# Third layer's projection in 64-row halves, with the group norm folded into its weights

## What is computed

```
def _L2_conv_ref(x, Wa1, ba1, Wa2, ba2, Wb1, bb1, Wb2, bb2, ln2_g, ln2_b, Wg, bg, Wz, bz):
    a = jax.nn.sigmoid((x @ Wa1 + ba1) * (x @ Wa2 + ba2))      # 64 -> 16 channels
    b = jax.nn.sigmoid((x @ Wb1 + bb1) * (x @ Wb2 + bb2))      # 64 -> 16 channels
    g = jax.nn.sigmoid(x @ Wg + bg)                            # 64 -> 64 channels
    z = jnp.einsum('bikc,bkjc->bijc', a, b)
    return g * (_ln(z, ln2_g, ln2_b) @ Wz + bz)
```

## Time and profile before

| | |
|---|---|
| median of 3 runs | 2089.22 us (2088.78 to 2090.52) |
| the profiled execution | 2091.39 us |
| its span (first to last instruction) | 2089.3 us |
| mean granted TensorE clock | 0.959 |
| busy: TensorE / VectorE / ScalarE / GpSimd | 1770.6 / 1319.1 / 1372.3 / 1031.0 us |
| fold of the third layer | about 1180 to 1189 us |
| projection of the third layer, first to last instruction | 1189.3 to 1311.0 us |

### The profile page before, as it was taken

One profiled execution on the slowest core, in us unless ns is written; L12 is line 12 of the kernel. 1 busy time (PEld: TensorE's weight loads), 2 busy tenths in 40 slices (PEclk: granted clock), 3 DMA queues, 4 the chain that ended last, 5 costly groups with the idle time before them and its releaser, 6 DMA issues. The chain is left out here.

```text
span 2089.3 us, 41026 instructions
## 1 busy us (share of the span) xinstructions
PE 1770.6 (85%) x10389; PEld 1045.5 (50%) x10389; DVE 1319.1 (63%) x2920; ACT 1372.3 (66%) x2541; POOL 1031.0 (49%) x1044
## 2 busy tenths in 40 slices
PE   0889997797998899985699799799799998699776
PEld 0444454685554444444355477643344444588533
DVE  7566666124763677775977388466377778344675
ACT  0577876365996777774599566477478787244554
POOL 0267678003991677786899200089122223000599
PEclk9999998898999999998899899999899999899999
DMA  7357876774996265647499666189557776845599
GB/s 327 124 184 236 245 232 216 271 297 169 365 367 235 97 189 168 193 135 264 146 357 366 231 226 207 35 321 385 175 157 227 237 236 216 296 174 228 193 398 373
DMA packets 326947, 496.15 MB, mean 237 GB/s; under 512 B 22828, under 2 KB 188463, under 8 KB 320439
## 3 DMA queue, kind: packets, MB, share of 16 engines
q1 hardware_dynamic: 326838, 494.93, 68.4%
HBM read 285.12 MB, written 197.13 MB: 231 GB/s over the span
## 5 line engine op out<-in xcount | busy, mean ns | idle before, releaser
L809 POOL TENSOR_TENSOR lo<-xn,hi 128x512 f16<-128x512 f32 x192 | 224.1, 1167 | 373.5 <-DVE hi L736 231.9
L601 PE MATMUL ps<-w_heads,hi 64*128 64x256 f16 x3072 | 292.8, 273 | 11.7 <-POOL lo L809 4.7
L1118 ACT ACTIVATE O<-ps 128x512 f32 (+1 forms) x144 | 151.7, 1054 | 189.3 <-PE ps L1042 189.3
L750 DVE SCALAR_TENSOR_TENSOR sig<-ps,largest,sig 128x512 f32<-128x512 f32 x256 | 180.7, 746 | 145.4 <-ACT sig L664 144.5
L664 ACT ACTIVATE sig<-ps,largest 128x512 f32<-128x512 f32 x384 | 246.1, 692 | 32.2 <-PE ps L601 23.3
L1355 POOL TENSOR_TENSOR shared<-O,out_rs 128x128 f32<-128x128 f32 (+1 forms) x112 | 76.3, 683 | 371.0 <-DVE out_rs L1255 370.0
L645 ACT ACTIVATE zs<-ps,shift 128x512 f32<-128x512 f32 x192 | 132.0, 687 | 192.9 <-PE ps L569 188.9
L601 PEld LDWEIGHTS ps<-w_heads,hi 64*128 64x128 f16 x3072 | 153.2, 95 | 169.3 <-DVE sig L750 67.0
L1403 PEld LDWEIGHTS ps<-ident,shared 128*128 128x128 f32 (+1 forms) x1024 | 120.2, 133 | 224.8 <-issue 96.8
L1403 PE MATMUL ps<-ident,shared 128*128 128x128 f32 (+1 forms) x1024 | 160.8, 282 | 76.6 <-POOL shared L1355 49.2
L601 PE MATMUL ps<-w_heads,lo 64*128 64x256 f16 x1536 | 212.8, 272 | 0.0
(11 more groups left out here) (168 smaller groups left out, 3787.6 us busy)
## 6 DMA issues: line engine op xcount, KB each, us to landing
shared<-left_right SPq DMA_DIRECT2D x34, 2048.0 KB, 12.0
shared<-gate SPq DMA_DIRECT2D x224, 256.0 KB, 4.6
gate<-gates SPq DMA_DIRECT2D x96, 512.0 KB, 2.9
x_dram<-shared SPq DMA_DIRECT2D x192, 256.0 KB, 4.3
shared<-x_dram SPq DMA_DIRECT2D x192, 256.0 KB, 4.7
xs<-x_dram SPq DMA_DIRECT2D x64, 512.0 KB, 4.2
left_right<-stage SPq DMA_DIRECT2D x64, 448.0 KB, 5.9
left_right<-shared SPq DMA_DIRECT2D x64, 448.0 KB, 5.9
```

What stands on the lines that cost most here:

```text
L601: last = pe.matmul(PAIR[row][:, g, kb * S:kb * S + S], tokens[half, q % 8, at:at + P], k["w_heads"][half, part, :], start=(step == 0), sto ...
L750: dve.scalar_tensor_tensor(dst, pair(row, 1), k["largest"][:, 1:2], factor, ALU.mult, ALU.mult).then_inc(pair_read.sem, 1)
L809: pool.tensor_tensor(lo[:, q % 8, :], xn[:, q % 2, :], hi[:, q % 8, :], ALU.subtract).then_inc(c["lo_done"].sem, 1)
L1118: act.activation(o_of(ch), ps[h % 4 // 2][:, h % 2, :].rearrange("p (b g i) -> p b g i", b=2, g=2), ACT.Copy).then_inc(c["o_copied"].sem, 1)
```

## The change

1. Token products as halves. The four products of 128 rows and 128 columns become eight of 64 rows and 64 columns: for each group of 128 tokens one with partitions 0 to 63 and one with 64 to 127, each half writing a PSUM bank of its own (`TILES` is now two half banks of `ps[0]` or of `ps[2]`). The weights' columns are reordered so that each 64 × 64 block stands on the diagonal, and the reads of L910 and L914 follow.
2. The affine step goes, with `xn` and its semaphore; TensorE reads `xs` itself and waits for its DMA. The slots of `xs` are now freed by the gate product.
3. The fold takes up scale and shift: `plain_weights` scales the weights' rows, and a new TensorE part `multiply_shift` multiplies the raw weights with the shift and adds the result to the projection's biases (a one-row product of 128 columns and a 128-row one into the same bank, instead of the 512-column one) and to the gate's bias (a one-column product). `plain_weights` now comes before the scaling of the output weights instead of after it.

```diff
+    def multiply_shift(self, pe):
+        k = self.k
+        pe.wait_ge(self.loaded.sem, self.loaded(16 * len(self.loads)))
+        pe.wait_ge(self.done.sem, self.done(7))
+        pe.matmul(self.P_PROJ[:, 0:P], k["one"][:], k["b_rows"][0:1, 0:P], start=True, stop=False)
+        pe.matmul(self.P_PROJ[:, 0:P], k["w_proj"][:, P:2 * P], k["w_raw"][:, 0:P], start=False, stop=True)
+        self.counted(pe.matmul(self.P_GATE[:, 0:1], k["w_raw"][:, CH:CH + P], self.shift, start=True, stop=True))

     def plain_weights(self, dve):
-        k, step, mm = self.k, self.step, self.mm
-        step(dve, dve.tensor_copy(k["w_proj"][:], k["w_raw"][:]))
+        k, step, mm, w = self.k, self.step, self.mm, self.k["w_proj"]
+        step(dve, dve.tensor_copy(w[:, P:2 * P], self.shift.to_broadcast([P, P])))
+        dve.wait_ge(self.loaded.sem, self.loaded(16 * len(self.loads)))
+        step(dve, dve.tensor_scalar(w[:, 0:P].rearrange("p (g x e) -> p g x e", g=2, x=2),
+                                    k["w_raw"][:, 0:P].rearrange("p (x g e) -> p g x e", g=2, x=2), self.scale, None, ALU.mult))
+        step(dve, dve.tensor_scalar(w[:, CH:CH + P], k["w_raw"][:, CH:CH + P], self.scale, None, ALU.mult))
         dve.wait_ge(mm.sem, mm(self.mm_of["plain_bias"]))
-        step(dve, dve.tensor_copy(k["mask"][:].rearrange("p g b i -> p (g b i)"), self.P_PROJ))
+        bias = self.P_PROJ[:, 0:P].rearrange("p (x g e) -> p g x e", g=2, x=2)
+        mask = k["mask"][:].rearrange("p g b i -> p (g b i)").rearrange("p (g t x e) -> p g t x e", g=2, t=4, x=2)
+        for g in range(2):
+            step(dve, dve.tensor_copy(mask[:, g], bias[:, g].unsqueeze(1).to_broadcast([P, 4, 2, P // 4])))
+        step(dve, dve.tensor_tensor(w[:, 2 * P:2 * P + 1], self.P_GATE[:, 0:1], k["vec"][:, V_GATE_B:V_GATE_B + 1], ALU.add))
...
-        xs, xn = sb("xs", [P, 8, CH]), sb("xn", [P, 4, CH])
-        TILES, GATE = [ps[0][:, q, :] for q in range(2)], [ps[1][:, q, :] for q in range(2)]
+        xs = sb("xs", [P, 8, CH])
+        TILES, GATE = [ps[bank][:, :, 0:S] for bank in (0, 2)], [ps[1][:, q, :] for q in range(2)]
...
-                sp.wait_ge(c["xn_done"].sem, c["xn_done"](m - 7))
+                sp.wait_ge(c["gate_mm_done"].sem, c["gate_mm_done"](m - 7))
...
-                    pe.wait_ge(c["xn_done"].sem, c["xn_done"](m + 1))
+                    load = c[f"x_in{q % 8}"]
+                    pe.wait_ge(load.sem, load(i * 32 + (q // 8 + 1) * 16))
                     pe.wait_ge(c["masked"].sem, c["masked"](m - 1))
                     for t in range(4):
-                        last = pe.matmul(TILES[q % 2][:, t * P:t * P + P], xn[:, q % 4, t * P:t * P + P],
-                                         k["w_proj"][:, 0:P], start=True, stop=True)
+                        for g in range(2):
+                            half = slice(g * C, g * C + C)
+                            last = pe.matmul(TILES[q % 2][:, g, t * C:t * C + C], xs[half, q % 8, t * P:t * P + P],
+                                             k["w_proj"][half, half], start=True, stop=True)
                     last.then_inc(c["proj_done"].sem, 1)
                     pe.wait_ge(c["gate_done"].sem, c["gate_done"](m - 1))
-                    pe.matmul(GATE[q % 2], k["w_proj"][:, CH:CH + P], xn[:, q % 4, :],
+                    pe.matmul(GATE[q % 2], k["w_proj"][:, CH:CH + P], xs[:, q % 8, :],
                               start=True, stop=True).then_inc(c["gate_mm_done"].sem, 1)
...
-                dve.tensor_tensor(biased[:, q % 2].rearrange("p a b -> p (a b)"), TILES[q % 2],
-                                  k["mask"][:].rearrange("p g b i -> p (g b i)"), ALU.add).then_inc(c["masked"].sem, 1)
+                dve.tensor_tensor(biased[:, q % 2].rearrange("p (g e) -> p g e", g=2), TILES[q % 2],
+                                  k["mask"][:].rearrange("p g b i -> p g (b i)"), ALU.add).then_inc(c["masked"].sem, 1)
...
-                dve.tensor_tensor(product[:, q % 2], biased[:, q % 2, :, 0:C], biased[:, q % 2, :, C:P],
+                factors = biased[:, q % 2].rearrange("p (g t x e) -> p x g t e", g=2, t=4, x=2)
+                dve.tensor_tensor(product[:, q % 2].rearrange("p t (g e) -> p g t e", g=2), factors[:, 0], factors[:, 1],
                                   ALU.mult).then_inc(c["sig_done"].sem, 1)
...
-            affine(0, 0)
-            affine(0, 1)
-            with dve.Fori(0, bodies - 1) as i:
+            with dve.Fori(0, bodies) as i:
                 for q in range(BODY):
-                    affine(i, q + 2)
                     multiply(i, q)
```

More of the change, by code:

```diff
@@ L185, in _ @@
                         fold.multiply_statistics(pe)
+                        fold.multiply_shift(pe)
                         fold.multiply_bias(pe)
@@ L193, in _ @@
                         fold.scale_and_shift(dve)
+                        fold.plain_weights(dve)
                         fold.scale_output(dve)
                         fold.take_output(dve)
-                        fold.plain_weights(dve)
                 fold.finish()
@@ L236, in __init__ @@
         self.mm_count, self.steps = 0, 0
-        order = (["mean", "var"] + (["shift"] if self.normed_in else []) + ["bias"] + ([] if self.normed_in else ["plain_bias"])
+        order = (["mean", "var"] + (["shift"] if self.normed_in else ["plain_bias"]) + ["bias"]
                  + ([] if self.masked else ["centered"]) + (["weights", "sizes", "largest"] if self.normed_in else []))
         self.mm_of = {name: at + 1 for at, name in enumerate(order)}
-        self.first = 8 if self.normed_in else 6
+        self.first = 8 if self.normed_in else 12
         self.out_scaled = self.first + (0 if self.masked else 2)
         self.weights_scaled, self.sized, self.on_diagonal = (self.out_scaled + at for at in (4, 10, 12))
-        self.all_steps = self.out_scaled + (23 if self.normed_in else 3)
+        self.all_steps = self.out_scaled + (23 if self.normed_in else 1)
         self.P_MEAN, self.P_VAR, self.P_SHIFT = ps[0][:, 0, :], ps[0][:, 1, :], ps[1][:, 0, :]
@@ L290, in multiply_bias @@
         self.counted(last)
-        if not self.normed_in:
-            self.counted(pe.matmul(self.P_PROJ, k["one"][:], k["b_rows"][0:1, 0:CH], start=True, stop=True))
+    def multiply_shift(self, pe):
[5 more added lines that the diff above has]
+        self.counted(pe.matmul(self.P_GATE[:, 0:1], k["w_raw"][:, CH:CH + P], self.shift, start=True, stop=True))
     def multiply_weights(self, pe):
@@ L845, in sb @@
             return ctx.enter_context(nc.sbuf_tensor(f"{name}_{n}", shape, dt))
-        xs, xn = sb("xs", [P, 8, CH]), sb("xn", [P, 4, CH])
-        biased, product, gates = sb("biased", [P, 2, 4, P]), sb("product", [P, 2, 4, C]), sb("gates", [P, 4, CH])
-        TILES, GATE = [ps[0][:, q, :] for q in range(2)], [ps[1][:, q, :] for q in range(2)]
+        xs = sb("xs", [P, 8, CH])
+        biased, product, gates = sb("biased", [P, 2, CH]), sb("product", [P, 2, 4, C]), sb("gates", [P, 4, CH])
+        TILES, GATE = [ps[bank][:, :, 0:S] for bank in (0, 2)], [ps[1][:, q, :] for q in range(2)]
         block = ctx.enter_context(nc.Block())
@@ L896, in _ @@
         def _(dve):
[L897 to L903, removed]
             def multiply(i, q):
@@ L949, in _ @@
                     act.activation(dst, GATE[q % 2], ACT.Sigmoid,
-                                   bias=k["vec"][:, V_GATE_B:V_GATE_B + 1]).then_inc(c["gate_done"].sem, 1)
+                                   bias=k["w_proj"][:, 2 * P:2 * P + 1]).then_inc(c["gate_done"].sem, 1)
     for s in range(8):
@@ L955, in project_plain @@
         c[f"gate_out{s}"].advance(16 * NCH // 8)
-    for name in ("xn_done", "proj_done", "masked", "sig_done", "lr_done", "gate_mm_done", "gate_done"):
+    for name in ("proj_done", "masked", "sig_done", "lr_done", "gate_mm_done", "gate_done"):
         c[name].advance(NCH)
```

## The result

| | before | changed |
|---|---|---|
| median | 2089.0 us (2086.0 to 2090.5, 4 runs) | 2219.5 us (2217.9 to 2224.6, 4 runs) |
| ratio, 95% interval | | 1.0631 (1.0609 to 1.0653) |
| span of the profiled execution | 2089.3 us | 2216.3 us |
| mean granted TensorE clock | 0.959 | 0.906 |

What follows compares the result with a forecast made beforehand. TensorE was taken to bound the projection loop, with VectorE little behind. Terms of 26.9 - 1.0 - 0.7 + 0.2 = + 25.4 us on 2091.4 gave 2116.8, and 2114.6 us as median; range 2085 to 2126.

Steps and rivals of the forecast that it cites:

- the sum: Projection loop's new period at full clock: tokens 0.93, gate 0.86 and switches 0.38 make 2.17 us against 1.75.
- (a): Loop's token products: halved streams but unchanged load times, 0.93 us an iteration against 0.89, so no gain.
- (c): The loop's gate product keeps its 0.86 us an iteration.
- R4: Rival on TensorE's clock: it falls to half throughout, the 2.17 us period doubles, about 2250 us; chance 0.02.
- (f): Weight fold ahead of the loop: TensorE and VectorE work changes, between - 0.5 and + 1.0 us, taken as + 0.2.
- R3: Rival on token products: loads of the two halves run serially, 3.00 us an iteration, 2168 us; chance 0.11.
- an offset of the halves: Token products: halves run offset by one pass, one round more less the shorter stream, + 0.05 us an iteration.
- (b): Switching between 64 and 128 rows in the loop: 0.19 us twice, 0.38 us an iteration.
- R2: Rival on the loop: comes out even through half-price loads (2085 us) or hidden switches (2090 us); chance 0.15.
- (d): Loop's VectorE loses the 0.54 us affine step, worth nothing; TensorE's 1.0 us wait for ScalarE vanishes, - 1.0 us.
- (e): Loop start: first product waits only for the load, no longer for the affine step, - 0.7 us.
- R1: Rival on the loop: real gain, half-price loads and free switches, 2059.5 us; chance 0.06.

Runs made afterwards that it cites:

- e3_warm: The changed kernel with eight dense f32 products of 512 columns ahead of its loop, results not used; 2109.9 us, ratio 1.0113.
- e5_pairs: The changed kernel with TensorE taking the token products of two chunks, then their gate products, halving the changes of rows; 2098.1 us, ratio 1.0042.
- e4_narrow_full: The changed kernel with each 64-column token product using all 128 rows, so no change of rows in the loop; 2141.4 us, ratio 1.0265.
- e2_wide: The changed kernel with each half product moving 128 columns instead of 64, the second 64 results not read; 2111.2 us, ratio 1.0120.
- e7_no_switch: The changed kernel with the gate product also as two 64-row halves, each in its own bank, read by two ScalarE instructions; 2111.9 us, ratio 1.0093.
- e1_fold_only: The changed kernel with its token products back to four of 128 rows and 128 columns; 2086.3 us, ratio 0.9995.
- e10_fold_warm: e1_fold_only with two dense f32 products of 512 columns ahead of its loop, in the wait for the first load; 2087.7 us, ratio 0.9995.
- e8: e4_narrow_full with 32 columns a product instead of 64, leaving out half of the projection's columns; 2301.2 us, ratio 1.1002.
- e12: e8 with eight dense f32 products of 512 columns ahead of its loop; 2150.7 us, ratio 1.0301.

## Why the prediction was wrong, and where it was right

**The step that failed** is the clock of the sum. (a) to (c) priced the new iteration at 1.00 for all 64 chunks, and R4, the rival "the clock falls", got 0.02. That was based on the earlier trace rows, where the first layer's loop alternates between 64 and 128 rows at 1.00. That row shows a loop holding the clock, with streams of 256 and 512 columns close behind each other. Mine entered at 0.50 and had to win it. The rows showed that too (L292, two passes in 2.05 us), and (f) even priced the fold at half clock, but I never asked when the clock rises after it and whether the changed iteration would still raise it. What the runs show in its place: 0.50 through all 64 iterations, 3.91 us each, 2219.5 us; and for the same loop entered at 1.00, 2.10 us each and 2109.9 us (e3_warm).

R4 had the direction and not the mechanism: the clock did not fall in the loop, it never rose. Its price, 2250, was 30 us too high. 4.34 us an iteration, twice the sum, is 0.43 more than 3.91: 0.14 is twice what the sum had too much at full clock, and 0.29 is that the switches do not double (3.91 is 0.41 over twice the 1.75 of before, against 0.35 at full clock).

**(a) The token products** were right in their mechanism: the halving gains nothing. The lines of e3_warm, shown above, and of e5_pairs tell what a round (one load and one pass of each half) takes. From the first token product to the gate product are 1261.19 − 1260.15 = 1.04 us for eight rounds, and in e5_pairs 1249.31 − 1247.38 = 1.93 us for sixteen. Eight rounds more cost 0.89 us, what the eight passes of the earlier trace rows cost.

```profile
1247.38 2.00 PE L909 MATMUL ps<-w_proj,xs 64*128 64x64 f32 x32
1249.31 1.99 PE L915 MATMUL ps<-xs,w_proj 128*128 128x512 f32 x4
1251.22 2.00 PE L909 MATMUL ps<-w_proj,xs 64*128 64x64 f32 x32
```

A load of 64 rows takes as long as one of 128. These are the shortest, the median and the longest load of e3_warm in ns, of the tokens and of the gate's weights:

```profile
L910 PEld LDWEIGHTS ps<-w_proj,xs x1024: 182/188/188, 1195.2 to 1327.9; 64*128 64x128 f32 x171
L914 PEld LDWEIGHTS ps<-xs,w_proj x128: 186/188/189, 1196.3 to 1328.3; 128*128 128x128 f32 x128
```

Sixteen such loads span 0.97 us in e3_warm, 7 × 0.11 + 0.19: two always run side by side, so R3 falls. One after the other they give e4_narrow_full's 2141 us. The streams of the halves overlap as well, which e2_wide shows: sixteen passes of 128 columns, 0.107 us of streaming each, would need 1.71 us in a row, and its whole iteration is 2.15. My + 0.05 for an offset of the halves was wrong.

**(b) The switches** were right in their mechanism, and a little too dear: 0.35 us for two and not 0.38. The same lines give it. 1.04 − 0.89 = 0.15 us are lost on the way to the gate product; two gate products take 1251.22 − 1249.31 = 1.91 us in e5_pairs and one takes 1262.25 − 1261.19 = 1.06 in e3_warm, so one more costs 0.85 and 0.21 are lost on the way back. Together that is 0.36. It agrees with three other differences: e3_warm's iteration is 0.35 longer than before, e7_no_switch's first ones, without any change of rows, are not longer at all, and e5_pairs, with half of the changes, gives back 0.18 a chunk (3.84 us for two). Rows 5 had 0.18 and 0.19, of which the prediction made 0.19 twice. The sign that I had named, idle before the tokens' first load put down to issue, shows at half clock and in e5_pairs:

```profile
L908 PEld LDWEIGHTS ps<-w_proj,xs x1024: 282/330/335, 1191.4 to 1439.0; 64*128 64x128 f32 x171
...
  issue: 98.8, 64
```

(changed kernel, us and times); in e3_warm it carries VectorE's name, as said above. R2 falls with both: the loads have their full price, and the switches are paid. The sum for full clock, 2.17 us an iteration, measured 2.10. That the time it gave, 2114.6, is near e3_warm's 2109.9 and e2_wide's 2111.2 is worth no more than a few us: the one holds eight added products, the other starts at half clock and streams more. The chip simply was not in that state.

**(d), (e), (f)** hold to a few tenths of a us. DVE's 0.54 us an iteration was worth nothing (e1_fold_only). From the fold's first instruction to the first load's issue are 9.36 us before and after, so the fold costs 0.0 where I took + 0.2. From there to the first token product are 3.27 us before and 2.87 after, − 0.4 where I took − 0.7. The 1.0 us of PE waiting for ACT is gone in the changed kernel and in e3_warm; e1_fold_only still has it.

**R1**, the gain, fell for the reason given against it. The Trainium skill (TensorEngine Tiling, Theoretical Speedup) allows up to 2× for products of at most 64 rows; here the streams of the halves do overlap, and yet at full clock the token products take 0.89 us as before, because with 64 moving columns the loads of 128 f32 columns set the pace, and the switches then cost 0.35.

The Trainium skill (TensorE: Matmul & The Clock Gate, "What's actually happening") says that the low clock is the default state and that activity releases it. The runs agree, and they show what a reader may miss in it: an engine that the profile calls busy 80 of 80 us was not active enough to be released for 250 us.

## What to carry to other kernels

An iteration that starts at half clock has to earn the full one: when a change makes TensorE's streams sparser (narrow moving sides, exposed loads, drains), look at the granted clock at the loop's entry, and ask whether the loop would win it, not whether a similar loop holds it. Where it would not, try a few dense products ahead of the loop: here they gave back 110 us net, though a loop that wins the clock by itself gained nothing from them (e10_fold_warm). And halving a product's rows and columns gains nothing where the stationary load, which took as long for 64 rows as for 128, is already as long as the stream.

## What the runs showed of the hardware

- The granted clock of one and the same loop can depend on the clock at which it is entered: 0.50 or 1.00 through 64 iterations (changed kernel and e3_warm; e8 and e12, the latter pair 150 us apart).
- Loads of stationary operands that fill most of the time did not raise the clock: e8 has PEld busy 63 of 80 us at 0.50.
- A load of 128 f32 columns over 64 rows lasts 0.19 us at full clock, as long as one over 128 rows, and two of them to different halves run side by side (sixteen in 0.97 us, e3_warm).
- Two changes between 64 and 128 rows cost 0.35 us an iteration in f32 at full clock (2.10 against 1.75 us; 1.75 again without them, in e7's first iterations), and 0.41 at half clock.

**Open.** Why the clock rises at different times in loops that win it (near 1198.2 us before and 1194.0 in e1_fold_only, whose first token products start at 1192.6 and 1191.1). How the chip weighs a stream of half rows against one of full rows: the runs tell that both narrower streams and more drains keep the clock down, not in what measure.
